# One overflow block of a mixture of experts moved from the end of the last stage to its start

## The chip, the cores and the metric

The kernel runs on one core of a Trainium2 chip. The metric is the device time of the whole kernel in microseconds (us). The engines are named as in the profile: PE is TensorE (PEld its weight loads), DVE is VectorE, ACT is ScalarE, POOL is GpSimd, SP is SyncE, which here only issues DMAs.

## What is computed

The kernel runs four pairs of attention and feed-forward layers on x, which is 2 batches of 1024 tokens of 256 numbers. Only the last feed-forward layer, a mixture of experts, is touched. Cut to what matters, it is:

```python
E, C, D, H = 8, 320, 256, 1024
xf = layernorm(x).reshape(2048, D)
eid = argmax(softmax(xf @ router_w + router_b), axis=-1)     # one expert for each token
rank = (cumsum(one_hot(eid), axis=0)[arange(N), eid] - 1)    # how many tokens before it chose the same expert
valid = rank < C                                             # an expert has room for 320 tokens
buf[eid, rank] = xf where valid
h = relu(einsum('ecd,edh->ech', buf, w1) + b1)
y = einsum('ech,ehd->ecd', h, w2) + b2
yov = relu(xf @ ow1 + ob1) @ ow2 + ob2                       # the tokens past 320 use this "overflow" network
out = where(valid, y[eid, rank], yov)
x = x + out
```

## The kernel before, in words

The tokens are held in SBUF as 16 tiles of 128 rows (the kernel calls a row of a tile with its token number, mean and reciprocal deviation behind it XW = 260 words). All of it is one program, stage after stage; the stage of this case is the last one, the function `moe3`. Its parts are written per engine, and each engine runs its part in the order written; semaphores tie them together. There is no scheduler.

**Routing.** The first twelve tiles (LAST = 12) are routed in earlier stages: their expert, their rank and their slot in a DRAM table `expert_rows` (`c.xd`) are known when the last stage starts. POOL has written the first eight of them into the table by then; at the head of the stage it writes tiles 8 to 11, one indirect DMA each (`scatter_tile`). The last four tiles must first be routed: PE transposes them (`ln_transpose`), multiplies them with the router's weights (`pe_logits`, L1172), brings the result back (`pe_logits_back`, L1181) and counts earlier tokens of each expert with bfloat16 matmuls of a matrix of ones (`pe_earlier_ranks`, `pe_count`, L1200; `pe_ranks`, L1215). DVE turns them into slots (`first_expert`, `slots`), and POOL then writes tiles 12 to 15. The table has 8 times 320 rows for the experts, and behind them, from row OV0 = 2560, rows for the overflow tokens of all experts, in the order of the tokens.

**The experts.** When all 16 scatters have landed, SP loads the table back (`load_x`, L2719, and `load_third`, L2725), then the second expert's weights (`load_w1`, `load_w2`), biases, more rows, the overflow rows (L2737) and the overflow network's weights `ow1` and `ow2` (L2740, L2741). PE runs nine matmuls whose result nobody reads (`keep_warm`, L110), transposes the rows (`x_transpose`, L2950) and then does for each of the eight experts `hidden` (L2963) and `outputs` (L2977), and after every second one `third_outputs` (L2986). ACT applies relu in between, DVE adds bias and residual (`finish`), POOL writes the result rows to the output in DRAM by an indirect DMA (`write`, L2769).

**The overflow blocks.** Behind the experts the overflow rows are computed in blocks of 128. A block is one `over_step` on PE: 16 matmuls with `ow1` (L3014), the next block's transposes (`over_transpose`, L2993) and 8 matmuls with `ow2` (L3025); DVE normalizes (`over_normal`, L2852), copies the transposed rows (`over_copy`, L2857) and finishes (`over_finish`); ACT does relu (`over_hidden`, L2914); POOL writes (`write_over`, L2781). Block 0 is written out in the program, and a loop with a count read at run time (`nbi`) does the rest, at least one more.

A matmul of float32 stands in the trace as two records: the 16 matmuls with `ow1` are 32 records.

Of the kernel before, what the change touches and what calls it, by code (L numbers as in the profile page):

```python
# [1146 lines left out]
def slots(c, dve, r, u, ranks, chain, read, nth=1):  # L1147
# [73 lines left out]
def scatter_tile(c, r, k):  # L1221
# [3 lines left out]
                                   in_=c.x[:, i * XW:(i + 1) * XW], in_offset=None).then_inc(c.scat, 16)  # L1225
# [1434 lines left out]
def moe3(c, d):  # L2660
# [4 lines left out]
    nbi = sb(c, "x_nbi", [1, 1], I32)  # L2665
    w1 = [c.early_w1, sb(c, "x_w11", [P, KC, HF])]
# [19 lines left out]
             "oy_set", "o_seen", "oy_ok", "o_out")  # L2686
# [15 lines left out]
    with nc.Block() as block:  # L2702
        @block.sync
        def _(sp):
# [3 lines left out]

            def load_w1(e):
# [16 lines left out]
            sp.wait_ge(c.scat, 16 * NT)  # L2726
# [6 lines left out]
            sp.dma_start(ob2[:, :], d["L3_ffn_ob2"].partition_broadcast(P)).then_inc(s["b_in"], 16)  # L2733
# [25 lines left out]
        def _(pool):  # L2759
# [4 lines left out]
            for k in range(LAST, NT):  # L2764
                scatter_tile(c, rt, k)
# [6 lines left out]
            for e in range(E3):  # L2772
                for r in range(2):
                    write(chunk(e, r), X[e % 4][:, r, D:D + 1].bitcast(U32))
                if e % 2 == 1:
                    write(third(e // 2), X3[e // 2 % 2][:, D:D + 1].bitcast(U32))

# [6 lines left out]
            write_over(0)  # L2784
            pool.wait_ge(s["nb_ok"], 1)
            nb = pool.value_load(nbi[0:1, 0:1], min_val=2, max_val=OVB)
            with pool.Fori(1, nb) as n:
# [409 lines left out]
```

## Time and profile before

| | before |
|---|---|
| runs (us) | 1004.54, 1004.16, 1007.02; median 1004.54 |
| the profiled execution: its time | 1005.3 us |
| its span, first to last instruction | 1003.5 us |
| mean granted clock of PE over the span | 0.968 |
| PE busy | 899.9 us, 90% of the span |
| last stage, from PE's first transposes | 803.4 to 1003.5 us |

The time of a run holds 1.8 us more than the span of the instructions. Times in the trace count from the span's start. The granted clock is the share of TensorE's full 2.4 GHz that was let through: 1.00 is 2.4 GHz and 0.50 is 1.2 GHz.

### The profile page before, as it was taken

How to read it: one execution, taken by the hardware profiler on the slowest of the kernel's cores; microseconds unless marked ns; L12 is line 12 of the kernel's file. 1: busy time of each engine (PE TensorE's matmuls, PEld its weight loads, DVE VectorE, ACT ScalarE, POOL GpSimd, SP SyncE). 2: the span in 40 equal slices, each digit the busy share in tenths (PEclk: the TensorE clock that was granted, in tenths of full speed). 3: DMA queues.
4: the chain of work that ended last, by engine and by line, in shares of the span. 5: the costliest groups of instructions: out<-in, count | busy, mean ns of one | idle time of the engine just before them, and what ended most of it. 6: DMA issues, size and time to landing. Idle time of an engine off the chain costs nothing. (4 is left out here: it accounts for less than half of the span.)

```text
span 1003.5 us, 17466 instructions
## 1 busy us (share of the span) xinstructions
PE 899.9 (90%) x5857; PEld 642.7 (64%) x5864; DVE 669.8 (67%) x1572; ACT 420.8 (42%) x1134; POOL 375.3 (37%) x279
## 2 busy tenths in 40 slices
PE   2899989999889995868899979999999949999997
PEld 2687744444478873744378647777777727778786
DVE  5899968889689988876377698787767531222221
ACT  2566641000146555752455336565655512122222
POOL 1776403333476732506545503333333430111111
PEclk9999999999899997987999999999999969999999
DMA  6100079999400007202356392311110149534200
GB/s 210 59 1 0 1 199 306 319 313 311 170 1 1 0 1 190 87 0 92 112 169 203 91 332 73 112 54 51 51 51 26 43 157 318 190 110 141 93 12 20
DMA packets 87259, 117.17 MB, mean 117 GB/s; under 512 B 12464, under 2 KB 75949, under 8 KB 86781
## 3 DMA queue, kind: packets, MB, share of 16 engines
q1 hardware_dynamic: 77455, 88.15, 29.1%
q10 hardware_dynamic: 4408, 15.46, 4.4%
q0 software_dynamic: 5328, 12.70, 3.5%
q8 instruction: 38, 0.62, 0.3%
q14 instruction: 30, 0.25, 0.1%
HBM read 68.08 MB, written 50.16 MB: 118 GB/s over the span
## 5 line engine op out<-in xcount | busy, mean ns | idle before, releaser
L1016 PE MATMUL psum<-m_W,lnT 128*128 128x512 f32 x256 | 114.2, 598 | 0.7 <-DVE acc L928 0.7
L410 POOL TENSOR_TENSOR prob<-prob,a_rden 128x1232 f32<-128x1232 f32 x30 | 67.5, 2249 | 58.4 <-DVE a_rden L506 58.4
L1016 PEld LDWEIGHTS psum<-m_W,lnT 128*128 128x128 f32 x256 | 47.2, 190 | 59.0 <-issue 56.5
L2907 ACT ACTIVATE prob<-psum,x_b 128x320 f32<-128x320 f32 x64 | 33.7, 527 | 117.1 <-PE psum L2963 117.1
L2574 PE MATMUL psum<-g_VW,pT 128*128 128x256 f32 (+1 forms) x320 | 72.5, 382 | 1.6 <-ACT pT L2461 1.5
L1001 POOL TENSOR_TENSOR m_masked<-m_rel,m_mrow 128x1232 f32<-128x1232 f32 x16 | 41.8, 2614 | 82.9 <-DMA masked_bias<-m_masked 62.0
L2769 POOL DMA_INDIRECT out_x<-x_yt,x_X x20 | 19.8, 991 | 135.3 <-DVE x_yt L2846 135.3
L2574 PEld LDWEIGHTS psum<-g_VW,pT 128*128 128x128 f32 (+1 forms) x320 | 59.5, 190 | 11.2 <-issue 3.7
L2232 POOL TENSOR_TENSOR g_qr<-g_t 128x1024 f32<-128x1024 f32 x15 | 35.4, 2359 | 71.1 <-DVE g_t L2305 71.1
L2239 POOL TENSOR_TENSOR prob<-prob,g_rden 128x1232 f32<-128x1232 f32 x15 | 33.7, 2247 | 67.6 <-DVE g_rden L2340 67.6
L2524 PE MATMUL psum<-g_Wq,lnT 128*128 128x512 f32 x128 | 58.0, 596 | 0.7 <-ACT lnT L2435 0.7
L1387 POOL DMA_INDIRECT routed_results<-pT,m_idx x39 | 38.3, 983 | 40.3 <-issue 23.5
L401 POOL TENSOR_SCALAR ln<-x_tiles,mean,rstd 128x256 f32<-128x256 f32 x32 | 41.4, 1294 | 30.6 <-DVE rstd L433 27.8
L2453 ACT ACTIVATE prob<-prob,mx 128x77 f32<-128x77 f32 x128 | 44.1, 347 | 19.0 <-DVE mx L2326 19.0
L472 DVE TENSOR_TENSOR prob<-psum,mx 128x616 f32<-128x616 f32 x64 | 48.2, 795 | 3.0
L466 DVE TENSOR_REDUCE mx<-psum 128x16 f32<-128x1232 f32 x32 | 45.6, 1424 | 4.7 <-PE psum L632 3.7
L962 ACT ACTIVATE lnT<-lnT_all 128x256 f32<-128x256 f32 x16 | 6.5, 415 | 95.2 <-PE psum L1023 95.2
L931 DVE SCALAR_TENSOR_TENSOR acc<-psum,gates,acc 128x256 f32<-128x256 f32 x96 | 40.3, 477 | 9.0 <-PE psum L1016 9.0
L549 ACT ACTIVATE prob<-prob 128x616 f32<-128x616 f32 x64 | 42.8, 713 | 6.1 <-DVE prob L472 6.1
L503 DVE TENSOR_REDUCE den<-prob 128x16 f32<-128x1232 f32 x30 | 42.8, 1427 | 3.6 <-ACT prob L549 3.2
L2843 DVE TENSOR_TENSOR x_yt<-psum,x_b 128x256 f32<-128x256 f32 (+1 forms) x24 | 10.2, 424 | 52.3 <-PE psum L2977 41.3
L1382 POOL DMA_INDIRECT routed_rows<-x_tiles,m_slot x32 | 31.8, 994 | 34.5 <-DVE m_slot L1575 25.3
(464 smaller groups left out, 2235.6 us busy)
## 6 DMA issues: line engine op xcount, KB each, us to landing
routed_rows<-hole SPq DMA_DIRECT2D x8, 2210.0 KB, 33.5
masked_bias<-m_masked ACTq DMA_DIRECT2D x16, 616.0 KB, 7.5
g_bias<-masked_bias SPq DMA_DIRECT2D x16, 616.0 KB, 3.8
m_xb<-routed_rows SPq DMA_DIRECT2D x39, 130.0 KB
m_rel<-in_rel_bias ACTq DMA_DIRECT2D x8, 616.0 KB, 9.6
expert_rows<-hole SPq DMA_DIRECT2D x1, 4680.0 KB, 32.4
g_early_w<-in_L_ffn_w SPq DMA_DIRECT2D x8, 512.0 KB, 4.6
g_early_w<-in_L_ffn_w SPq DMA_DIRECT2D x4, 1024.0 KB, 5.9
```

The lines of the kernel that those rows point to most:

```text
L401: nc.gpsimd.tensor_scalar(c.ln[b][:, :], xt(c, i), mean_of(c, i), rstd_of(c, i), ALU.subtract, ALU.mult).then_inc(ln_ok, 1)
L410: nc.gpsimd.tensor_tensor(heads(c.prob[b]), heads(c.prob[b]), rden[b][:, :].unsqueeze(2).to_broadcast([P, H, SK]), ALU.mult).then_inc(norm ...
L466: nv.reduce_max(c.mx[:, :].rearrange("p (r h) -> p r h", r=GROUPS), sview.rearrange("p r (h k) -> p r h k", k=SK), AX).then_inc(mx_ok, 1)
L472: nv.tensor_tensor(c.prob[b].rearrange("p (r h k) -> p r h k", r=GROUPS, k=SK)[:, r], sview[:, r].rearrange("p r (h k) -> p r h k", k=SK), ...
L503: nv.reduce_sum(c.den[:, :], heads(c.prob[b]), AX).then_inc(den_ok, 1)
L549: na.activation(c.prob[b][:, cols], c.prob[b][:, cols], ACT.Exp, scale=scale).then_inc(exp_ok, 1)
L931: ins = nv.scalar_tensor_tensor(out=c.acc[o][:, :], in0=src, scalar=gate, in1=c.acc[o][:, :], op0=ALU.mult, op1=ALU.add)
L1001: nc.gpsimd.tensor_tensor(masked[i % 2][:, :, :], rel[i // 2 % 2][:, :, :], mrow[:, i % 2, :].unsqueeze(1).to_broadcast([P, HB, SK]), ALU. ...
L1016: last = nt.matmul(c.ps[p][:, :], c.lnT[b][:, k * P:(k + 1) * P], W[:, k, p * 512:(p + 1) * 512], start=(k == 0), stop=(k == KC - 1))
L2453: last = na.activation(p, p, ACT.Exp, bias=c.mx[:, h:h + 1], accum_out=c.den[:, h:h + 1])
L2524: last = nt.matmul(c.ps[3 + u][:, :], c.lnT[b][:, k * P:(k + 1) * P], Wq[:, k, u * 512:(u + 1) * 512], start=(k == 0), stop=(k == KC - 1))
L2574: last = nt.matmul(bank_y[:, 0:D], c.pT[b][0:w, j * P:(j + 1) * P], VW[0:w, i // HALF, j, :], start=(j == 0), stop=(j == NB - 1))
```

## The change

The first overflow block is computed ahead of the experts. Its 128 rows are loaded into a tile of its own, `Xe`, as soon as the first twelve tiles are in the table; the last four tiles count on a semaphore of their own. The overflow network's weights and the bias `ob2` are loaded at the head of the stage. So that the first block is closed when tiles 12 to 15 are placed, PE also counts the experts' tokens in the first twelve tiles (12 more small matmuls; all its counts of earlier tiles now stand ahead of the logits), and DVE works out how many of the block's 128 rows they leave free (`free`); the overflow rows of the last four tiles begin behind the block (`start`). The matmuls of `keep_warm` at this place are gone. The loop of the other blocks begins at block 2, behind a block 1 that is written out, so at least three blocks are computed.

```diff
@@ -1157,9 +1157,9 @@
...
-    chain(nv.tensor_tensor(slotf, slotf, over, ALU.subtract))
+    chain(nv.scalar_tensor_tensor(out=slotf, in0=slotf, scalar=free, in1=over, op0=ALU.subtract, op1=ALU.subtract))
     chain(nv.scalar_tensor_tensor(out=slotf, in0=rank, scalar=float(CAP), in1=slotf, op0=ALU.is_lt, op1=ALU.mult))
-    return nv.scalar_tensor_tensor(out=r.slot[:, ones8], in0=slotf, scalar=float(E3 * CAP), in1=over, op0=ALU.add, op1=ALU.add)
+    return nv.scalar_tensor_tensor(out=r.slot[:, ones8], in0=slotf, scalar=start, in1=over, op0=ALU.add, op1=ALU.add)
...
     for shift in shifts:
-        pe_count(c, r, u, bank, shift, max(lo, shift), min(lo + wide, lo + shift), start=shift == shifts[0])
+        last = pe_count(c, r, u, bank, shift, max(lo, shift), min(lo + wide, lo + shift), start=shift == shifts[0])
+    if wide > n:
+        for j in range(lo):
+            last = c.nc.tensor.matmul(bank[:, wide * 8:(wide + 1) * 8], r.onesb, r.ohb[:, j * 8:(j + 1) * 8],
+                                      start=False, stop=True, skip_group_check=True)
+    return last
...
             sp.dma_start(ob1[:, :], d["L3_ffn_ob1T"]).then_inc(s["w_in"], 16)
+            sp.dma_start(ob2[:, :], d["L3_ffn_ob2"].partition_broadcast(P)).then_inc(s["w_in"], 16)
+            for k in range(KC):
+                sp.dma_start(ow1[:, k, :], d["L3_ffn_ow1"][k * P:(k + 1) * P, :]).then_inc(s["ow_in"], 16)
+            sp.dma_start(ow2[:, :, :], d["L3_ffn_ow2"].rearrange("(m p) n -> p m n", p=P)).then_inc(s["ow_in"], 16)
...
-            sp.wait_ge(c.scat, 16 * NT)
+            sp.wait_ge(c.scat, 16 * LAST)
+            sp.dma_start(Xe[:, :], xd[OV0:OV0 + P, :]).then_inc(s["first_in"], 16)
+            sp.wait_ge(s["scat"], 16 * (NT - LAST))
             load_x(0)
             load_third(0)
...
-            sp.dma_start(ob2[:, :], d["L3_ffn_ob2"].partition_broadcast(P)).then_inc(s["b_in"], 16)
...
                          xd[OV0:OV0 + OVX * P, :].rearrange("(r p) n -> p r n", p=P)).then_inc(s["ox_in"], 16)
-            for k in range(KC):
-                sp.dma_start(ow1[:, k, :], d["L3_ffn_ow1"][k * P:(k + 1) * P, :]).then_inc(s["ow_in"], 16)
-            sp.dma_start(ow2[:, :, :], d["L3_ffn_ow2"].rearrange("(m p) n -> p m n", p=P)).then_inc(s["ow_in"], 16)
...
-                scatter_tile(c, rt, k)
+                scatter_tile(c, rt, k, s["scat"])
...
-            for e in range(E3):
-                for r in range(2):
...
             write_over(0)
+            for e in range(E3):
+                for r in range(2):
...
+
+            write_over(1)
             pool.wait_ge(s["nb_ok"], 1)
-            nb = pool.value_load(nbi[0:1, 0:1], min_val=2, max_val=OVB)
-            with pool.Fori(1, nb) as n:
+            nb = pool.value_load(nbi[0:1, 0:1], min_val=3, max_val=OVB)
+            with pool.Fori(2, nb) as n:
...
             dve_rstd(c, dve, chain, s["ve_ok"], s["std_ok"])
+            dve.wait_ge(s["early_ps"], 1)
+            chain(nv.tensor_scalar(over8[:, :], bank_rank[:, (NT - LAST + 1) * 8:(NT - LAST + 2) * 8], -float(CAP), 0.0, ALU.add, ALU.max))
+            chain(nv.reduce_sum(free[:, 0:1], over8[:, :], AX))
+            chain(nv.tensor_scalar(free[:, 0:1], free[:, 0:1], -1.0, float(P), ALU.mult, ALU.add))
+            nv.tensor_scalar(start[:, :], free[:, 0:1], 0.0, float(OV0), ALU.max, ALU.add)
+            chain(nv.tensor_scalar(free[:, 1:2], free[:, 0:1], 0.0, None, ALU.max))
...
+            slots(c, dve, rt, 2, bank_rank, chain, s["pre_read"], 1, free[:, 1:2], start[:, 0:1]).then_inc(s["slot_ok"], 1)
+            dve.wait_ge(s["w_in"], 16 * 4)
...
+            chain(nv.tensor_tensor(nbf[:, 0:1], nbf[:, 0:1], start[0:1, :], ALU.add))
...
+            nv.tensor_scalar(nbi[:, :], nbf[:, 1:2], 3.0, None, ALU.max).then_inc(s["nb_ok"], 1)
...
-            def over_rows(n):
-                return Xo[:, ds(n * XW, D)]
+            def over_rows(n, at=0, wide=D):
+                return Xe[:, at:at + wide] if is_static(n) and n == 0 else Xo[:, ds(n * XW + at, wide)]
...
+            def over_finish(n):
+                dve.wait_ge(s["oy_ps"], n + 1)
...
+            dve.wait_ge(s["first_in"], 16)
+            over_normal(0)
+            over_copy(0)
             normal_rows(0)
             x_copy(0)
+            over_finish(0)
             for e in range(E3):
                 if e + 1 < E3:
...
-                    over_normal(0)
-                    over_copy(0)
+                    over_normal(1)
+                    over_copy(1)
...
-            over_step(0)
-            nb = dve.value_load(nbi[0:1, 0:1], min_val=2, max_val=OVB)
-            with dve.Fori(1, nb) as n:
+            over_step(1)
+            nb = dve.value_load(nbi[0:1, 0:1], min_val=3, max_val=OVB)
+            with dve.Fori(2, nb) as n:
                 over_step(n)
...
-            act.wait_ge(s["w_in"], 16 * 3)
-            for e in range(E3):
-                if e >= 2:
-                    wait(act, s["y_ps"], third(e // 2 - 1) + 1)
...
+            act.wait_ge(s["w_in"], 16 * 4)
...
             over_hidden(0)
+            for e in range(E3):
+                if e >= 2:
...
+            over_hidden(1)
             act.wait_ge(s["nb_ok"], 1)
-            nb = act.value_load(nbi[0:1, 0:1], min_val=2, max_val=OVB)
-            with act.Fori(1, nb) as n:
+            nb = act.value_load(nbi[0:1, 0:1], min_val=3, max_val=OVB)
+            with act.Fori(2, nb) as n:
...
                 ln_transpose(n, k)
+            pe_earlier_ranks(c, rt, 2, bank_rank).then_inc(s["early_ps"], 1)
             pe.wait_ge(s["lnT_ok"], NT - LAST)
             pe_logits(c, rt, 2, bank_lg).then_inc(s["lg_ps"], 1)
             pe.wait_ge(s["lgT_ok"], 1)
             pe_logits_back(c, rt, 2, bank_back).then_inc(s["logits_ps"], 1)
-            pe_earlier_ranks(c, rt, 2, bank_rank)
...
@@ -2968,6 +2990,8 @@
                 b = e % 2
                 if e > 0:
                     pe.wait_ge(w2_in[b], 16 * ((e + 1) // 2))
+                if e == 0:
+                    pe.wait_ge(s["oy_ok"], 1)
...
-            pe.wait_ge(c.scat, 16 * NT)
-            keep_warm(c, c.ps[3], 9)
-            x_transpose(0)
-            for e in range(E3):
-                hidden(e)
-                if e + 1 < E3:
...
-                    over_transpose(0)
-                outputs(e)
...
-            pe.wait_ge(s["ow_in"], 16 * (KC + 1))
-
             def over_step(n):
+                early = is_static(n) and n == 0
...
-                over_transpose(n + 1)
+                if not early:
+                    over_transpose(n + 1)
                 wait(pe, s["oy_ok"], n)
-                if is_static(n):
+                if is_static(n) and not early:
...
+            over_transpose(0)
+            pe.wait_ge(s["ow_in"], 16 * (KC + 1))
             over_step(0)
+            x_transpose(0)
+            for e in range(E3):
+                hidden(e)
+                if e + 1 < E3:
...
+                    over_transpose(1)
+                outputs(e)
...
+            over_step(1)
             pe.wait_ge(s["nb_ok"], 1)
-            nb = pe.value_load(nbi[0:1, 0:1], min_val=2, max_val=OVB)
-            with pe.Fori(1, nb) as n:
+            nb = pe.value_load(nbi[0:1, 0:1], min_val=3, max_val=OVB)
+            with pe.Fori(2, nb) as n:
                 over_step(n)
```

On PE at the start of the stage stand before the change (names: `lnT_all` the transposed tiles, `qT` here the router's weights, `oT` the logits, `lg` the tokens' choices, `choice` the matrix of ones):

```order
L1172 MATMUL psum<-lnT_all,qT 32x256 x4
L1181 MATMUL psum<-ident,oT 128x64 x2
L1200 MATMUL psum<-lg,choice 128x40 x8
L1200 MATMUL psum<-lg,choice 128x8
L1200 MATMUL psum<-lg,choice 128x16
```

and after it, at the same place:

```order
L1200 MATMUL psum<-lg,choice 128x16
L1200 MATMUL psum<-lg,choice 128x8
L1212 MATMUL psum<-lg,choice 128x8 x12
L1172 MATMUL psum<-lnT_all,qT 32x256 x4
L1181 MATMUL psum<-ident,oT 128x64 x2
L1220 MATMUL psum<-lg,choice 128x32
```

The counts of earlier tiles (16 matmuls) have moved from behind the logits to ahead of them, and 12 more follow them (L1212).

A little further on PE, between the ranks and the first expert, stand before the change (`RQ,identb` is `keep_warm`, `x_XL` the experts' normalized rows, `x_xT` the same transposed, `g_early_w` the first expert's weights, `prob` its hidden layer):

```order
L1200 MATMUL psum<-lg,choice 128x8
L110 MATMUL psum<-RQ,identb 128x512 x9
L2950 MATMUL psum<-ident,x_XL 128x128 x6
L2963 MATMUL psum<-x_xT,g_early_w 128x320 x16
L2950 MATMUL psum<-ident,x_XL 128x128 x4
```

and after it (`oT` are now the overflow block's rows, `x_ow` its weights, `Wall` its hidden layer):

```order
L1200 MATMUL psum<-lg,choice 128x8
L3017 MATMUL psum<-ident,oT 128x128 x2
L3025 MATMUL psum<-oT,x_ow 128x128 x16
L3037 MATMUL psum<-x_ow,Wall 128x256 x8
L2972 MATMUL psum<-ident,x_XL 128x128 x6
L2985 MATMUL psum<-x_xT,g_early_w 128x320 x16
```

The block has taken the place of the nine `keep_warm` matmuls, between the ranks and the first expert's transposes.

SP issues these DMAs from the head of the stage before the change (`x_X` are the experts' rows, `x_w` the second expert's weights, `x_tiles` here the tile of the overflow rows):

```order
L2705 DMA x_steps<-in_c_steps 1x14
L2706 DMA x_b<-in_L_ffn_b1T 128x64
L2707 DMA x_ob<-in_L_ffn_ob1T 128x8
L2719 DMA x_X<-expert_rows 128x2x260
L2725 DMA x_X<-expert_rows 64x260 x2
L2719 DMA x_X<-expert_rows 128x2x260
L2711 DMA x_w<-in_L_ffn_w 128x1024 x2
L2715 DMA x_w<-in_L_ffn_w 128x8x256
L2732 DMA x_b<-in_L_ffn_b 128x2048
L2733 DMA x_ob<-in_L_ffn_ob 128x256
```

and after it:

```order
L2712 DMA x_steps<-in_c_steps 1x14
L2713 DMA x_b<-in_L_ffn_b1T 128x64
L2714 DMA x_ob<-in_L_ffn_ob1T 128x8
L2716 DMA x_ob<-in_L_ffn_ob 128x256
L2718 DMA x_ow<-in_L_ffn_ow 128x1024 x2
L2719 DMA x_ow<-in_L_ffn_ow 128x8x256
L2739 DMA x_Xe<-expert_rows 128x260
L2731 DMA x_X<-expert_rows 128x2x260
L2737 DMA x_X<-expert_rows 64x260 x2
L2731 DMA x_X<-expert_rows 128x2x260
```

The overflow network's bias and weights stand ahead of all loads of rows, and the load of the block's rows ahead of the experts' first.

## Rows read from the trace of the kernel before

**Rows 1.** The page: busy time, share of the span, number of instructions.

```profile
PE 899.9 (90%) x5857; PEld 642.7 (64%) x5864; DVE 669.8 (67%) x1572; ACT 420.8 (42%) x1134; POOL 375.3 (37%) x279
```

**Rows 2.** Waits of 796 to 840 us: who waited for what, us, times, longest.

```profile
DVE x_XL L2823 <- DMA x_X<-expert_rows: 9.3, 1, 9.3
PE psum L110 <- DMA expert_rows<-x_tiles,acc: 8.4, 1, 8.4
```

**Rows 3.** Timeline of PE, stage start: start us, us busy, what, idle before it.

```profile
803.41 1.32 PE L2932 MATMUL psum<-ident,x_tiles 128*128 128x128 f32 x8 [1.62 <-PEq L175]
805.20 1.71 PE L1172 MATMUL psum<-lnT_all,qT 128*32 128x256 f32 x8 [0.47 <-ACT lnT_all L2896]
807.79 0.64 PE L1200 MATMUL psum<-lg,choice 128*128 128x40 bf16 x16
...
818.22 3.62 PE L110 MATMUL psum<-RQ,identb 128*128 128x512 bf16 x8 [8.36 <-DMA expert_rows<-x_tiles,acc]
822.75 0.88 PE L2950 MATMUL psum<-ident,x_XL 128*128 128x128 f32 x6 [0.91 <-DVE x_XL L2823]
...
840.99 8.78 PE L2963 MATMUL psum<-x_xT,x_w 128*128 128x320 f32 x32
```

**Rows 4.** The chain that ended last, in order of time, same place.

```profile
815.34 2.43 DMA expert_rows<-x_tiles,acc
...
818.75 2.77 DMA x_X<-expert_rows
821.63 1.07 DVE x_XL L2823 x3
```

**Rows 5.** Timeline of PE, end of the kernel: the overflow blocks.

```profile
968.25 3.84 PE L3014 MATMUL psum<-oT,x_ow 128*128 128x128 f32 x32
...
982.84 3.73 PE L3014 MATMUL psum<-oT,x_ow 128*128 128x128 f32 x32
986.41 0.38 PE L2993 MATMUL psum<-ident,oT 128*128 128x128 f32 x2
986.63 3.62 PE L3025 MATMUL psum<-x_ow,Wall 128*128 128x256 f32 x16
990.08 3.73 PE L3014 MATMUL psum<-oT,x_ow 128*128 128x128 f32 x32
```

**Rows 6.** Timeline of POOL and DVE, stage start and last block.

```profile
807.81 0.96 POOL L1224 DMA_INDIRECT expert_rows<-x_tiles,acc  x1 [0.31 <-issue]
...
812.18 0.14 DVE L2808 TENSOR_SCALAR x_nbi<-x_nbf 1x1 int32<-1x1 f32 x1
...
991.67 0.41 DVE L2852 TENSOR_SCALAR oT<-x_tiles 128x256 f32 x1 [0.23 <-issue]
...
994.07 0.42 DVE L2857 COPY oT<-psum 128x256 f32<-128x256 f32 x1 [2.00 <-PE psum L2993]
997.62 0.42 DVE L2877 TENSOR_TENSOR qT<-psum,x_ob 128x256 f32<-128x256 f32 x1 [3.12 <-PE psum L3025]
...
998.25 0.43 DVE L2881 TENSOR_TENSOR qT<-qT,x_tiles 128x256 f32<-128x256 f32 x1
```

**Rows 7.** Timeline of SP's queue: issues of DMAs.

```profile
804.09 0.42 SPq L2707 DMA_DIRECT2D x_ob<-in_L_ffn_ob1T  x1
...
820.02 0.94 SPq L2711 DMA_DIRECT2D x_w<-in_L_ffn_w  x2
821.01 0.43 SPq L2715 DMA_DIRECT2D x_w<-in_L_ffn_w  x1
...
822.49 0.88 SPq L2733 DMA_DIRECT2D x_ob<-in_L_ffn_ob  x1
```

**Rows 8.** DMA issues, 803 to 842 us, then 618 to 650 us: KB each, us to landing.

```profile
x_w<-in_L_ffn_w SPq DMA_DIRECT2D x1, 1024.0 KB, 8.5
...
g_early_w<-in_L_ffn_w SPq DMA_DIRECT2D x1, 1024.0 KB, 6.4
```

**Rows 9.** L2769's 20 indirect DMAs, then L2719's 8 loads, min/median/max.

```profile
DMA to landing us min/median/max: 2.1/2.4/5.9
...
DMA to landing us min/median/max: 2.7/8.3/10.3
```

**Rows 10.** Windows: length, busy of PE, PEld, DVE, ACT, POOL; PE's granted clock, DMA share, GB/s.

```profile
805.20:809.90 4.70, 3.05 (x31) 1.54 (x31) 1.75 (x11) 0.43 (x2) 2.88 (x3) 0.53 0.33 117
809.90:818.20 8.30, 0.00 (x0) 0.13 (x2) 2.08 (x14) 0.00 (x0) 3.83 (x4) 0.50 0.18 65
818.20:822.50 4.30, 3.62 (x8) 1.06 (x7) 0.87 (x3) 0.00 (x0) 0.00 (x0) 0.50 0.78 214
822.50:825.00 2.50, 0.92 (x7) 0.71 (x7) 1.53 (x6) 0.00 (x0) 0.00 (x0) 0.99 0.95 326
```

More of the change, by code:

```diff
@@ L1144, in first_expert, with slots @@
     return nv.tensor_tensor(tiles(hot), tiles(tmp), wide(first), ALU.is_equal)
-def slots(c, dve, r, u, ranks, chain, read, nth=1):
+def slots(c, dve, r, u, ranks, chain, read, nth=1, free=0.0, start=float(E3 * CAP)):
     nv = c.nc.vector
@@ L1218, in pe_ranks, with scatter_tile @@
     return last
-def scatter_tile(c, r, k):
+def scatter_tile(c, r, k, done=None):
     i = TOKEN_ORDER[k]
     c.nc.gpsimd.indirect_dma_start(out=c.xd, out_offset=bass.IndirectOffsetOnAxis(ap=r.slot[:, k:k + 1], axis=0),
-                                   in_=c.x[:, i * XW:(i + 1) * XW], in_offset=None).then_inc(c.scat, 16)
+                                   in_=c.x[:, i * XW:(i + 1) * XW], in_offset=None).then_inc(done or c.scat, 16)
 def row_statistics(c, u):
@@ L2665, in moe3 @@
     nbi = sb(c, "x_nbi", [1, 1], I32)
+    over8, free, start = sb(c, "x_over8", [P, 8]), sb(c, "x_free", [P, 2]), sb(c, "x_start", [P, 1])
+    Xe = sb(c, "x_Xe", [P, XW])
     w1 = [c.early_w1, sb(c, "x_w11", [P, KC, HF])]
@@ L2784, in _ @@
             write_over(0)
+            for e in range(E3):
+                for r in range(2):
+                    write(chunk(e, r), X[e % 4][:, r, D:D + 1].bitcast(U32))
+                if e % 2 == 1:
+                    write(third(e // 2), X3[e // 2 % 2][:, D:D + 1].bitcast(U32))
+            write_over(1)
             pool.wait_ge(s["nb_ok"], 1)
-            nb = pool.value_load(nbi[0:1, 0:1], min_val=2, max_val=OVB)
-            with pool.Fori(1, nb) as n:
+            nb = pool.value_load(nbi[0:1, 0:1], min_val=3, max_val=OVB)
+            with pool.Fori(2, nb) as n:
                 write_over(n)
@@ L2857, in over_copy @@
                 nv.tensor_copy(xTo[:, :], c.ps[0][:, 0:D]).then_inc(s["oT_ok"], 1)
+            def over_finish(n):
+                dve.wait_ge(s["oy_ps"], n + 1)
+                wait(dve, s["o_out"], n * 16)
+                nv.tensor_tensor(yo[:, :], c.ps[6][:, 0:D], ob2[:, :], ALU.add).then_inc(s["oy_set"], 1)
+                nv.tensor_copy(ido[:, :], over_rows(n, D, 1).bitcast(U32))
+                wait(dve, s["o_seen"], n)
+                dve.wait_ge(s["oy_set"], n + 1)
+                nv.tensor_tensor(yo[:, :], yo[:, :], over_rows(n), ALU.add).then_inc(s["oy_ok"], 1)
+            dve.wait_ge(s["first_in"], 16)
+            over_normal(0)
+            over_copy(0)
             normal_rows(0)
             x_copy(0)
+            over_finish(0)
             for e in range(E3):
@@ L2873, in _ @@
                     finish(third(e // 2), [(e - 1, slice(0, C2)), (e, slice(C2, P))], rows_of(e - 1, 2))
-            def over_finish(n):
-                dve.wait_ge(s["oy_ps"], n + 1)
-                wait(dve, s["o_out"], n * 16)
-                nv.tensor_tensor(yo[:, :], c.ps[6][:, 0:D], ob2[:, :], ALU.add).then_inc(s["oy_set"], 1)
-                nv.tensor_copy(ido[:, :], Xo[:, ds(n * XW + D, 1)].bitcast(U32))
-                wait(dve, s["o_seen"], n)
-                dve.wait_ge(s["oy_set"], n + 1)
-                nv.tensor_tensor(yo[:, :], yo[:, :], over_rows(n), ALU.add).then_inc(s["oy_ok"], 1)
             def over_step(n):
@@ L2900, in _ @@
             logits_copy(c, rt, 2, bank_lg).then_inc(s["lgT_ok"], 1)
-            act.wait_ge(s["w_in"], 16 * 3)
-            for e in range(E3):
-                if e >= 2:
-                    wait(act, s["y_ps"], third(e // 2 - 1) + 1)
-                for m in range(MH):
-                    act.wait_ge(s["h_ps"], e * MH + (m + 1))
-                    na.activation(hT[e % 2][:, m, :], c.ps[2 + m % 4][:, 0:CAP], ACT.Relu,
-                                  bias=b1[:, e * MH + m:e * MH + m + 1]).then_inc(s["h_ok"], 1)
+            act.wait_ge(s["w_in"], 16 * 4)
             def over_hidden(n):
@@ L2917, in _ @@
             over_hidden(0)
+            for e in range(E3):
+                if e >= 2:
+                    wait(act, s["y_ps"], third(e // 2 - 1) + 1)
+                for m in range(MH):
+                    act.wait_ge(s["h_ps"], e * MH + (m + 1))
+                    na.activation(hT[e % 2][:, m, :], c.ps[2 + m % 4][:, 0:CAP], ACT.Relu,
+                                  bias=b1[:, e * MH + m:e * MH + m + 1]).then_inc(s["h_ok"], 1)
+            over_hidden(1)
             act.wait_ge(s["nb_ok"], 1)
-            nb = act.value_load(nbi[0:1, 0:1], min_val=2, max_val=OVB)
-            with act.Fori(1, nb) as n:
+            nb = act.value_load(nbi[0:1, 0:1], min_val=3, max_val=OVB)
+            with act.Fori(2, nb) as n:
                 over_hidden(n)
```

21 lines of the change are left out of this document (7 added, 14 removed).

## The prediction

> **What bounds the kernel now.** I read the page first: PE is busy for 90% of the span [rows 1], so the question is where PE is not busy, and what PE does that could be done there. The waits around the start of the last stage show the hole: PE waits 8.4 us for the scatters into the table, and DVE 9.3 us for the rows loaded back [rows 2]. The timeline shows it from PE's side: after the ranks (about 809.9) PE does nothing until `keep_warm` at 818.22, and that is work nobody reads; the first transposes of the experts start at 822.75 [rows 3]. The chain of the end says why: the last scatter starts at 815.34 and lands 2.43 us later, the last load starts at 818.75 and lands 2.77 us later, DVE normalizes for 1.07 us, and PE goes on [rows 4]. From there to the end PE waits for nobody for long. At the end it computes four overflow blocks, one every 990.08 - 982.84 = 7.24 us [rows 5]. So the kernel's end is PE's work from 822.75 on: a block taken from there is worth 7.24 us, less what it pushes 822.75 back.
>
> **The removed block.** The trace has four blocks: the first of `ow1`'s groups is at 968.25, the last at 990.08, (990.08 - 968.25) / 7.24 = 3 steps after the first [rows 5]. So between 385 and 512 tokens overflow. The change fills its block only if the first twelve tiles alone overflow by 128 or more; rows they leave free would be added to the rest, and a fifth block would come. Counting the choices of the reference's router on its inputs gives 472 overflow tokens, 215 of them in the first twelve tiles. The first block is then full, nothing is left free, and (472 - 128) / 128 rounds up to 3 blocks behind the experts. Term one: **-7.24 us**. Block 1 takes block 0's place in the program and the tail behind the last block stays what it was.
>
> **Moved and added counts.** PE now does the 16 counts of earlier tiles and 12 more ahead of the logits. 16 took 0.64 us [rows 3], so 28 take 28 x 0.04 = 1.12 us. They start when the tiles' transposes end, at 803.41 + 1.32 = 804.73, and end at 805.85, where the logits started at 805.20: 0.65 us late. Before, the 16 lay in PE's wait for DVE and cost nothing. DVE waits for PE's logits behind them, then come the slots, POOL's four scatters, SP's loads: all 0.65 us late. The five new small DVE instructions (about 0.2 us each, like the one at 812.18 [rows 6] and its neighbours) stand ahead of that wait, while DVE would wait anyway, and cost nothing. So the experts' rows let PE begin at 822.75 + 0.65 = 823.4 at the earliest. Term two is this 0.65 us only if the block is done by then.
>
> **When the block can start.** It needs its rows and its weights. SP is free at 804.09 + 0.42 = 804.51; the bias takes 0.88 us to issue, `ow1` 0.94, `ow2` 0.43 [rows 7] (by DMAs of the same shape elsewhere), so `ow2` is issued from about 806.4. A 1 MB load behind others of its kind lands 8.5 us after its issue, one with little ahead of it 6.4 us [rows 8]: 812.8 to 814.9. I take 8.5 us, since the bias and 1 MB of `ow1` are right ahead: 814.9. Tile 12's scatter starts at 807.81 [rows 6] and lands 2.43 us later [rows 4] at 810.2 if the weights leave it alone. SP issues the load of the block's rows (0.4 us), which takes 2.77 us [rows 4]: 813.4 alone. It is behind `ow2` in SP's queue, so I take 815.0. DVE has finished its counts by 812.18 + 0.14 + 0.65 = 813.0 [rows 6] and is no limit. Then 0.1 us to wake DVE, 0.41 us to normalize [rows 6], 0.05 us to PE: PE transposes from 815.6.
>
> **How long it takes there.** At the end of the kernel the block costs 7.24 us because its transposes and copy hide under the block before. Here they don't: from the start of the transposes to the end of the copy it is 994.07 + 0.42 - 993.65 = 0.84 us (the transposes at 993.65 are 7.24 us behind those at 986.41 [rows 5]; the copy is in [rows 6]). I add 0.3 us for the wake-up and the slower clock: `ow1` starts at 816.7. The rest is 986.41 - 982.84 = 3.57 us and 990.08 - 986.63 = 3.45 us, 7.02 us at full clock [rows 5]. But PE has idled, and its granted clock is 0.50 (1.2 GHz) from 805.2 to 822.5; it rose to 2.4 GHz 4.3 us after `keep_warm` began [rows 10]. The same 4.3 us from 815.6 give 819.9. From 816.7 to 819.9 PE does 3.2 / 2 = 1.6 us of the 7.02; the other 5.42 us end at 825.3. Then the experts' transposes start, their rows long there: 825.3 - 822.75 = 2.55 us later than before. Term two is therefore **+2.55 us**, and the 0.65 us are inside it. `keep_warm` needs no replacement: the block warms the clock itself.
>
> **What is free.** `ow1`, `ow2` and `ob2` in SP's later queue are gone, which only frees DMA. The second expert's weights now land at about 821.01 + 8.5 + 0.65 = 830.2 [rows 7, 8] and are wanted after 840.99 [rows 3]. DVE finishes the block between the first expert's copy and the second's rows: 998.25 + 0.43 - 997.62 = 1.06 us [rows 6], with the second expert's transposes wanted some 9 us later. The first expert's `outputs` wait for this finish, also some 9 us later; POOL writes the block while it has nothing else. ACT's relu of the block lies under PE's matmuls as it does at the end.
>
> **The sum.** -7.24 + 2.55 = -4.7 us, of which I give 0.2 for wake-ups I have not counted: -4.5. On the profiled execution's own time of 1005.3 us that is 1000.8; it was 0.8 us above the median of 1004.54, so against the median I say 1000.0.
>
> The loads at the head speak against this change. The nearest row is POOL's writes to the output, of which the slowest took 5.9 us to land and the median 2.4 [rows 9], the slow one among heavy loads; by it tile 12 lands at 813.7, the rows at 816.9 and not 815.0, and 1.9 us of the gain are lost, -2.6 us. The Trainium skill (DMA: Bandwidth & Descriptors, Issuing engines are not separate DMA queues) says that DMAs of all issuing engines run on the same 16 DMA engines and interleave, and its section on queues, rings and completion order that a DMA engine takes the queues in turn, packet by packet. By that a scatter gets its turn beside the weights: my estimate from the page is at most twice its 2.43 us, tile 12 at 812.7, the rows at 815.9, and a sum of -3.6 us.
>
> **The rivals.**
> - *The block hides almost whole.* The weights land after 6.4 us, scatter and load as if alone: rows at 813.4, 1.6 us sooner, block done at 823.7 against the 823.4 of the experts' own rows. -7.24 + 0.95 = -6.3 us: 998.2 (997.9 if only the 0.65 us are left). For it: the DMA share is only 0.33 at 805.2 to 809.9 [rows 10]. Against it: 2 MB are added just there. 0.14.
> - *Rows or clock late.* The slow scatter above, or a clock that rises later: were it at 1.2 GHz during the whole block, the block would take 14.0 us to 830.7, and the sum would be +0.7 us. Between: 0 to -3 us, 1001.6 to 1004.5, say 1002.5. For it: the block's transposes and the wait for the copy are thinner work than `keep_warm`. 0.20.
> - *Slower: the block's rows are stuck behind the weights.* Loads from the table took up to 10.3 us, 8.3 in the median, when the queue was full [rows 9]. It decides where the rows land after 815.0 + (7.24 - 2.55) = 819.7, for then PE has lost more at the front than it saved at the end; with a scatter of 5.9 and a load of 10.3 us they land at 807.81 + 5.9 + 0.4 + 10.3 = 824.4, +4.7 us: 1009.3. Against it: such loads stood in a queue that kept the DMA engines 0.95 busy [rows 10], and this one has 2 MB ahead of it. 0.08, half of it by over 0.3%.
> - *The change does not do what it says*: five blocks in all, so +2.55 us: 1007.1. The counts above speak against it. 0.02.
> - My forecast, -3 to -6 us: 0.56.
>
> **The numbers.** 0.3% is 3.0 us, about what can be told from no change. Faster by more than that are the forecast and the first rival: 0.70. Within it the second and half of the third: 0.24. Slower 0.06. The range from 998.2 to 1003.6 leaves out the end of the first rival, the slow third of the second and the last two.
>
> **What would show it.** Right: three groups of `ow1` matmuls at the end, 7.24 us apart, and one of about 5 us between 816 and 822, in which the spacing halves half-way; the block's rows landing at about 815; the first experts' transposes at about 825.3, hidden work 2.2 us behind as before. Wrong: PE waiting for the block's rows beyond 817 (scatter or load late), or for the weights with the rows transposed; a granted clock of 0.50 into the `ow2` matmuls; four groups still at the end; a wait of PE in the first two experts, which would mean that DVE's or POOL's new order costs something.

## The result, and the profile after

The changed kernel takes 1001.39 us in the median of 20 runs, the kernel before 1006.46 us in as many: a ratio of 0.9958, 95% interval 0.9944 to 0.9971. That is 4.2 us less (2.9 to 5.6); the two medians by themselves lie 5.1 us apart, which is inside this interval. The trace's own execution took 999.59 us, with a span of 997.8 us.

Single runs of one kernel differ by several us here (before: 1001.4 to 1010.3), and part of that arises before the last stage. The two traces differ by 5.7 us in their spans, but 4.2 us of it are there when the last stage begins: PE's first transposes of the stage are at 803.41 before [rows 3] and at 799.17 after. That difference comes in earlier, where nothing was changed: PE's work of the same name is 0.3 us apart in the two traces at 467 us, 4.24 us at 580.6 us, and it stays so from there on. So below, times are given as distances from the stage's first transposes, which I call the stage's start. By that the first pair of traces says: last stage 200.1 us before, 198.6 us after, a gain of 1.5 us only.

The waits around the start of the last stage, after (us in total, times, longest):

```profile
PE psum L3017 <- DVE oT L2869: 9.5, 1, 9.5
...
DVE oT L2869 <- DMA x_Xe<-expert_rows: 6.4, 1, 6.4
```

PE's wait of [rows 2] is no shorter; it has a new cause, DVE's normalizing of the early block, and behind that the load of its rows. PE's timeline of the same trace, against [rows 3]:

```profile
799.17 1.32 PE L2954 MATMUL psum<-ident,x_tiles 128*128 128x128 f32 x8 [1.63 <-PEq L175]
...
800.33 0.55 PE L1200 MATMUL psum<-lg,choice 128*128 128x40 bf16 x16
...
800.74 0.44 PE L1212 MATMUL psum<-lg,choice 128*128 128x8 bf16 x12
...
801.11 1.06 PE L1172 MATMUL psum<-lnT_all,qT 128*32 128x256 f32 x8
...
814.44 0.69 PE L3017 MATMUL psum<-ident,oT 128*128 128x128 f32 x2 [9.48 <-DVE oT L2869]
...
815.74 5.37 PE L3025 MATMUL psum<-oT,x_ow 128*128 128x128 f32 x32 [0.61 <-DVE oT L2874]
820.94 3.62 PE L3037 MATMUL psum<-x_ow,Wall 128*128 128x256 f32 x16
824.40 0.82 PE L2972 MATMUL psum<-ident,x_XL 128*128 128x128 f32 x6
```

The experts' first transposes are 824.40 - 799.17 = 25.2 us behind the stage's start, where they were 822.75 - 803.41 = 19.3. I call this distance the front; it has grown by 5.9 us. Why the block starts late is in the timelines of POOL, SP and DVE:

```profile
803.58 0.96 POOL L1229 DMA_INDIRECT expert_rows<-x_tiles,acc  x1 [0.30 <-issue]
...
810.11 0.33 SPq L2739 DMA_DIRECT2D x_Xe<-expert_rows  x1
...
813.97 0.41 DVE L2869 TENSOR_SCALAR oT<-x_Xe 128x256 f32<-128x256 f32 x1 [6.38 <-DMA x_Xe<-expert_rows]
...
818.58 1.06 DVE L2840 TENSOR_SCALAR x_XL<-x_X 128x256 f32<-128x256 f32 x3 [2.99 <-DMA x_X<-expert_rows]
```

The block's rows wait for the last of the first twelve tiles. (The prediction calls it tile 12; counted from 0, as in the kernel, it is tile 11. I call it the twelfth tile.) Its scatter starts at 803.58, 4.4 us behind the stage's start as in [rows 6], but SP, which waits for it, issues its load only at 810.11. The chain that ended last has the two durations:

```profile
803.58 6.52 DMA expert_rows<-x_tiles,acc
...
810.11 3.84 DMA x_Xe<-expert_rows
```

The scatter took 6.5 us where 2.43 [rows 4] had done. The experts' own rows are there at 818.58 + 1.06 = 819.6 and wait almost 5 us for PE. The windows (busy of PE, PEld, DVE, ACT, POOL, then granted clock, DMA share, GB/s) put the block's two halves at the two clocks:

```profile
810.00:814.00 4.00, 0.00 (x0) 0.00 (x0) 0.03 (x1) 0.00 (x0) 1.23 (x2) 0.50 0.73 260
...
814.00:819.00 5.00, 3.95 (x17) 3.58 (x18) 1.23 (x4) 0.00 (x0) 0.00 (x0) 0.50 0.65 181
819.00:824.40 5.40, 5.40 (x36) 4.94 (x35) 0.63 (x2) 2.28 (x8) 0.00 (x0) 1.00 0.92 317
```

And the end, against [rows 5], has three blocks where there were four, 7.35 and 7.25 us apart:

```profile
969.83 3.84 PE L3025 MATMUL psum<-oT,x_ow 128*128 128x128 f32 x32
...
977.18 3.73 PE L3025 MATMUL psum<-oT,x_ow 128*128 128x128 f32 x32
...
984.43 3.73 PE L3025 MATMUL psum<-oT,x_ow 128*128 128x128 f32 x32
```

From the experts' first transposes to the end it is 1003.5 - 822.75 = 180.8 us before and 997.8 - 824.40 = 173.4 us after. I call this the rest. Rest -7.4, front +5.9: -1.5 us. The question for the experiments was where the other 2.7 us of the timed 4.2 are.

### The profile page after: what moved, and what is told of

Same layout as the page of the kernel before. It is cut to its first block and busy times, and to the rows that moved or that the text cites. A ratio compares the mean times of both kernels' runs of the same rounds, so it can differ in the third digit from the quotient of the medians.

```text
span 997.8 us, 17467 instructions
## 1 busy us (share of the span) xinstructions
PE 896.7 (90%) x5867; PEld 644.1 (65%) x5867; DVE 668.5 (67%) x1577; ACT 420.4 (42%) x1134; POOL 375.3 (38%) x279
## 5 line engine op out<-in xcount | busy, mean ns | idle before, releaser
L1392 POOL DMA_INDIRECT routed_results<-pT,m_idx x39 | 38.4, 984 | 39.3 <-DVE pT L1725 19.8
L931 DVE SCALAR_TENSOR_TENSOR acc<-psum,gates,acc 128x256 f32<-128x256 f32 x96 | 40.6, 476 | 10.8 <-PE psum L1016 10.7
L660 PE MATMUL psum<-pT,a_VB 128*32 128x128 f32 x1088 | 40.9, 275 | 3.4 <-ACT pT L555 3.4
```

## The experiments

All ratios are to the kernel before, timed on the same chip. Front and rest come from each kernel's own trace.

| kernel | front | rest | last stage | ratio (95%) |
|---|---|---|---|---|
| before | 19.3 | 180.8 | 200.1 | 1 |
| before_again | 18.5 | 184.1 | 202.5 | 0.9992 (0.9972 to 1.0012) |
| before_third | 19.3 | 180.8 | 200.0 | 0.9994 (0.9971 to 1.0018) |
| changed | 25.2 | 173.4 | 198.6 | 0.9958 (0.9944 to 0.9971) |
| after_again | 24.9 | 173.4 | 198.3 | 0.9964 (0.9947 to 0.9981) |
| after_third | 24.8 | 173.4 | 198.2 | 0.9954 (0.9932 to 0.9976) |
| weights_first | 18.8 | 183.7 | 202.5 | 1.0000 (0.9985 to 1.0014) |
| one_fewer | 19.4 | 175.2 | 194.6 | 0.9933 (0.9909 to 0.9957) |
| before_warm_long | 19.4 | 182.5 | 201.9 | 0.9990 (0.9971 to 1.0009) |
| warm | 25.0 | 173.3 | 198.3 | 0.9949 (0.9929 to 0.9970) |
| warm_long | 24.8 | 173.4 | 198.2 | 0.9965 (0.9934 to 0.9996) |
| swap | 23.3 | 173.4 | 196.7 | 0.9946 (0.9927 to 0.9965) |
| swap_again | 22.2 | 173.5 | 195.7 | 0.9946 (0.9920 to 0.9972) |
| swap_warm | 22.4 | 175.9 | 198.3 | 0.9951 (0.9930 to 0.9973) |

### The two kernels again

*before_again* and *before_third* are the kernel before, *after_again* and *after_third* the changed kernel, with no edit.

> The kernel before, unchanged, for a second trace. The first pair of traces puts 1.5 us of the gain in the last stage (200.1 us before, 198.6 us after, from PE's first transposes of the stage to the end) and 4.2 us ahead of it, in stages that the change does not touch. Theory 1 (the stages ahead differ from execution to execution whatever the kernel): ratio 1.000; the last stage again 200.1 us within 0.5, the stages ahead up to 4 us away from 803.4. Theory 2 (the last stage itself varies, by the phase of the clock or the landing of the scatters): the last stage differs by 1 us or more from 200.1.

> The changed kernel, unchanged, for a second trace. Theory 1 (the front of the last stage is always lengthened by 5.9 us, so the stage gains 1.5 us, and what the medians show beyond that comes from ahead of the stage): last stage 198.6 us within 0.5, first transposes of the experts 25.2 us behind the stage's. Theory 2 (the front varies; the first trace shows a bad case): that distance between 22 and 25 us, last stage 196 to 198 us. Ratio to before 0.996 in both.

> The kernel before, unchanged, for a third trace. Theory A (the nine matmuls of keep_warm and the thin work behind them do not hold the clock at 1.00 through the first expert in every execution): the part from the experts' first transposes to the end is 182.5 to 184 us in this one, as in four of the five traces so far that have keep_warm and four blocks or one fewer (taken with 7.24 us more), and the last stage lasts 202 us or so. Rival (the first trace is the usual case): 180.8 us and 200.1 us. Ratio 1.000.

> The changed kernel, unchanged, for a third trace. Theory A: the part from the experts' first transposes to the end is 173.3 to 173.4 us again, since a whole block of dense work stands ahead of them, and the front is 24.9 to 25.3 us. Rival (that it was at full clock each time is chance): over 174.5 us. Ratio 0.996.

For the changed kernel theory 1 was right: its stage is steady (198.6, 198.3, 198.2) and its front too. For the kernel before both theories hold: its last stage began at 799.8 us in the second trace and at 803.4 in the other two, and its length varies (200.1, 202.5, 200.0), which was theory 2. In the first trace, the first expert's hidden layer:

```profile
824.96 8.85 PE L2963 MATMUL psum<-x_xT,g_early_w 128*128 128x320 f32 x32 [1.34 <-DVE x_xT L2832]
```

The second trace, timeline of PE (cut off at 832 us, so with 31 of the 32 records):

```profile
813.53 4.02 PE L110 MATMUL psum<-RQ,identb 128*128 128x512 bf16 x9 [8.10 <-DMA expert_rows<-x_tiles,acc]
818.25 1.54 PE L2950 MATMUL psum<-ident,x_XL 128*128 128x128 f32 x6 [0.70 <-DVE x_XL L2823]
821.13 11.17 PE L2963 MATMUL psum<-x_xT,g_early_w 128*128 128x320 f32 x31 [1.33 <-DVE x_xT L2832]
```

and its windows:

```profile
817.00:822.00 5.00, 2.97 (x10) 1.85 (x9) 2.85 (x9) 0.00 (x0) 0.00 (x0) 0.50 0.98 331
822.00:826.00 4.00, 4.00 (x8) 2.49 (x8) 0.00 (x0) 0.76 (x2) 0.00 (x0) 0.50 1.07 400
826.00:828.00 2.00, 2.00 (x8) 1.46 (x7) 0.00 (x0) 0.82 (x2) 0.00 (x0) 0.91 0.98 256
```

`keep_warm` ran, and yet the clock stayed at 0.50 until after 826: the transposes took 1.54 us instead of 0.88, the first expert's whole hidden layer 11.4 us instead of 8.85. The experts' rows were early in this execution (front 18.5, not 19.3), but the rest is 3.3 us longer. In the third trace the clock was up in time again, so my expectation of a low clock there was a miss. The changed kernel's rest is 173.4 us in all three; a whole block of dense matmuls stands ahead of its first expert, which I take for the reason, though no run isolates it.

### The weights alone at the head

```diff
             sp.dma_start(ob1[:, :], d["L3_ffn_ob1T"]).then_inc(s["w_in"], 16)
+            for k in range(KC):
+                sp.dma_start(ow1[:, k, :], d["L3_ffn_ow1"][k * P:(k + 1) * P, :]).then_inc(s["ow_in"], 16)
+            sp.dma_start(ow2[:, :, :], ...).then_inc(s["ow_in"], 16)
...
-            for k in range(KC):
-                sp.dma_start(ow1[:, k, :], ...)
-            sp.dma_start(ow2[:, :, :], ...)
```

> The kernel before with one part of the change: the overflow network's weights loaded at the head of the stage (the bias stays where it was); the four blocks stay at the end. Theory 1 (2 MB at the head hold up the scatters): the scatter of the twelfth tile lands 6 us after its start instead of 2.4, the last one up to 2 us later than before, and the experts' first transposes start 1 to 2 us later; ratio 1.001 to 1.002. Rival (the scatters of the last four tiles come when the weights are nearly through): no delay, ratio 1.000.

The ratio is 1.0000 (0.9985 to 1.0014). The last scatters are through at the same time: SP issues the experts' first load 13.8 us behind the stage's start, in before_again 13.7. The rival was right: by themselves the weights cost the kernel before nothing that shows, 0.3 us of front at most (18.8 against 18.5). What it waits for is the last of the 16 scatters, and that starts at 810.98, when the weights are nearly through (`ow2` lands at 811.3), and takes 2.7 us. What they cost the changed kernel is the early block's own rows, which come while they are under way. This trace, too, has the first expert's beginning at the low clock (again 31 of its 32 records):

```profile
818.62 1.54 PE L2950 MATMUL psum<-ident,x_XL 128*128 128x128 f32 x6 [0.92 <-DVE x_XL L2823]
821.49 10.87 PE L2963 MATMUL psum<-x_xT,g_early_w 128*128 128x320 f32 x31 [1.33 <-DVE x_xT L2832]
```

### One block fewer

The kernel before without its last block; 88 overflow tokens are not computed.

```diff
-            nv.tensor_scalar(nbi[:, :], nbf[:, 1:2], 2.0, None, ALU.max).then_inc(s["nb_ok"], 1)
+            nv.tensor_scalar(nbi[:, :], nbf[:, 1:2], -1.0, 2.0, ALU.add, ALU.max).then_inc(s["nb_ok"], 1)
```

> The kernel before with one overflow block fewer behind the experts: the count of the run-time loop is lowered by one, so the last block (88 of the 472 overflow tokens) is left out. Theory (a block at the end is worth its whole 7.24 us): the part from the experts' first transposes to the end shrinks by 7.2 to 7.3 us, ratio 0.9928. Rival (part of the block hides under the tail of POOL's writes or under the experts): less than 6.5 us, ratio above 0.9935.

The ratio of 0.9933 is 6.7 us less (4.3 to 9.1), and holds 7.24. The rest is 175.2 us, 5.5 us less than the first trace's, not 7.2: here the clock fell back to 0.50 for some 3.4 us inside the first expert, whose hidden layer took 10.5 us and not 8.85:

```profile
828.17 10.54 PE L2963 MATMUL psum<-x_xT,g_early_w 128*128 128x320 f32 x32 [1.33 <-DVE x_xT L2832]
```

The blocks at the end of this trace are 7.24 us apart, and one is gone:

```profile
980.50 3.73 PE L3014 MATMUL psum<-oT,x_ow 128*128 128x128 f32 x32
...
987.74 3.73 PE L3014 MATMUL psum<-oT,x_ow 128*128 128x128 f32 x32
```

### Idle PE kept busy

*warm* (the changed kernel) and *swap_warm* (below) have the first piece, *warm_long* both, *before_warm_long* the second alone.

```diff
+            pe.wait_ge(c.scat, 16 * LAST)
+            keep_warm(c, c.ps[3], 9)
             over_transpose(0)
...
             pe_ranks(c, rt, 2, bank_rank).then_inc(s["pre_ps"], 1)
+            keep_warm(c, c.ps[3], 20)
```

> The changed kernel with nine matmuls that nobody reads put between the first twelve tiles' landing and the early block, where PE is idle. Theory 1 (the block is slowed by the clock of 0.50 in its first 4.6 us): the block's matmuls run at 1.00 almost from the start, it ends 1.6 to 2.3 us sooner against the stage's start, and the time falls by as much, ratio to before about 0.994. Rival (the block's end is set by weights that land late): the block ends where it did and the ratio stays at 0.996.

> The kernel before with 20 matmuls that nobody reads right behind the ranks, where PE waits 8 us for the scatters; the nine of keep_warm stay. Theory A (what the gain shows beyond 1.5 us is that the kernel before starts its first expert at the low clock in part of its executions, as its second trace shows, 21.4 to 26.4 us behind the stage's start, and the changed one never does): with PE busy the clock is at 1.00 before the first expert in every execution; the part from the experts' first transposes to the end is 180.8 us or less, never 184, and the ratio is 0.997 to 0.999. Rival (that second trace is rare): the ratio is 1.000.

> The changed kernel with 20 matmuls that nobody reads right behind the ranks and nine more when the first twelve tiles have landed. Theory (the early block is slow only by the clock of 0.50 in its first 3.4 to 4.8 us): the clock does not fall or is back at 1.00 before the block, the ow1 matmuls take 3.7 us instead of 5.4 to 5.7, the experts' first transposes start 22.8 to 23.3 us behind the stage's start instead of 24.9 to 25.2, ratio 0.994. Rival (the clock falls in spite of it, or the 20 matmuls at the low clock delay the block): 24.9 us or more, ratio 0.996 or above.

None of the three did what I wanted. In *warm* the nine matmuls filled the last 4 us of the gap and the clock rose no sooner: at about 20.0 us behind the stage's start (799.56), 19.8 in the changed kernel. Its windows:

```profile
808.00:812.00 4.00, 1.70 (x5) 0.59 (x6) 0.00 (x0) 0.00 (x0) 3.02 (x4) 0.50 1.05 384
812.00:816.00 4.00, 3.39 (x10) 1.31 (x9) 0.84 (x2) 0.00 (x0) 0.00 (x0) 0.50 0.38 117
816.00:819.00 3.00, 3.00 (x16) 3.00 (x16) 0.66 (x3) 0.00 (x0) 0.00 (x0) 0.50 0.90 251
819.00:820.00 1.00, 1.00 (x8) 1.00 (x8) 0.40 (x2) 0.57 (x3) 0.00 (x0) 0.72 0.91 344
```

The front is 25.0 us as without them. The expectation's rival, weights that land late, is not the reason either: `ow2`, issued at 802.31, landed 10.4 us later, at 812.7, and PE's first matmul with the weights is at 815.58. The ratio of 0.9949 overlaps that of the changed kernel, so it is no gain that I can show. In *warm_long* the block ran at the full clock (`ow1` in 3.65 us), but the result of PE's logits reached ACT 2.5 us late in that trace and the 29 matmuls, done at 820.8, stood in front of the block: front 24.8, no gain. *before_warm_long* had the clock up before the first expert, and then lost it during the expert, right behind the two waits of 2.52 and 1.33 us for the rows: rest 182.5, and a ratio of 0.9990. So theory A's first half stands (the kernel before has its first expert partly at the low clock in three of the five traces without the 20 matmuls, and in this one), and my remedy for it fails. That the waits right ahead of the expert would have to be filled instead is what this suggests; it was not tried.

### The two sets of weights exchanged

The stage before has room for one set of weights in advance, and used it for the first expert. Here the overflow network's get it, and the first expert's are loaded in the last stage, behind the early block's rows.

```diff
-                sp.dma_start(c.early_w1[:, k, :], d["L3_ffn_w1"][k * P:(k + 1) * P, :]).then_inc(c.early_in, 16)
+                sp.dma_start(c.early_w1[:, k, :], d["L3_ffn_ow1"][k * P:(k + 1) * P, :]).then_inc(c.early_in, 16)
...
-    w1 = [c.early_w1, sb(c, "x_w11", [P, KC, HF])]
-    ow1, ow2 = sb(c, "x_ow1", [P, KC, HF]), sb(c, "x_ow2", [P, MH, D])
+    w1 = [sb(c, f"x_w1{u}", [P, KC, HF]) for u in range(2)]
+    ow1, ow2 = c.early_w1, c.early_w2
...
             sp.dma_start(Xe[:, :], xd[OV0:OV0 + P, :]).then_inc(s["first_in"], 16)
+            load_w1(0)
+            load_w2(0)
```

> The changed kernel with the two sets of weights exchanged: the overflow network's are loaded in the stage before, in the place of the first expert's, and the first expert's are loaded in the last stage right behind the block's rows. Theory (the rows of the block are late because the 2 MB at the head delay the scatter of tile 12 from 2.4 to 6.5 us and the load from 2.8 to 3.8): the load is issued 6.9 to 7.1 us behind the stage's start instead of 10.7 to 10.9, DVE has the rows at 10.0 to 10.5 instead of 14.2 to 14.8, the block ends 3 to 4 us sooner, at 21 to 22, and the experts' first transposes follow there. If the first expert's weights are then in time, ratio 0.993; the rival is that they are not, or hold up the last scatters, and the experts start no sooner than 24 us, ratio 0.996.

> The kernel with the two sets of weights exchanged, unchanged, for a second trace and time. In its first trace the front was 23.3 us, and PE's results of the router reached DVE and ACT 2.8 us late, for which nothing in the trace accounts. If that is an accident of one execution, the logits' copy starts about 3.0 us behind the stage's start instead of 6.4; the front stays at 22.5 to 23.3 us, since the block's rows do not hang on it; ratio 0.994 to 0.995. If it is of this kernel, it comes again.

> The kernel with the two sets of weights exchanged and nine matmuls that nobody reads behind the landing of the first twelve tiles. Theory (in the exchanged kernel what is left of the front is the block at the low clock, 1.5 to 3 us): the block ends up to 2 us sooner, front 21 to 22.5 us, ratio 0.992 to 0.994. Rival (as in the kernel with nine such matmuls and the weights in the old order, the clock does not rise sooner for them): front 23.3 us, ratio as without them.

SP's queue in swap_again (stage's start 799.80):

```profile
806.67 0.33 SPq L2736 DMA_DIRECT2D x_Xe<-expert_rows  x1
807.04 0.91 SPq L2720 DMA_DIRECT2D x_w<-in_L_ffn_w  x2
807.99 0.43 SPq L2724 DMA_DIRECT2D x_w<-in_L_ffn_w  x1
817.13 0.38 SPq L2728 DMA_DIRECT2D x_X<-expert_rows  x1
```

and PE's timeline there:

```profile
809.23 0.69 PE L3012 MATMUL psum<-ident,oT 128*128 128x128 f32 x2 [3.63 <-DVE oT L2868]
810.53 6.33 PE L3020 MATMUL psum<-oT,g_early_w 128*128 128x128 f32 x32 [0.61 <-DVE oT L2873]
816.70 3.62 PE L3032 MATMUL psum<-g_early_w,Wall 128*128 128x256 f32 x16
822.04 0.88 PE L2971 MATMUL psum<-ident,x_XL 128*128 128x128 f32 x6 [1.73 <-DVE x_XL L2839]
```

With no weights under way the scatter of the twelfth tile has landed 6.9 us behind the stage's start instead of 10.7 to 10.9 (2.5 us after its start and not 6.3 to 6.5), and the load of the block's rows takes 2.1 us instead of 3.4 to 3.8, so their lateness is shown to be the weights'. The block starts at 9.4 us and is done at 20.5. Now the experts' own rows are last: their load is issued at 17.3 us, in the changed kernel at 15.0 to 15.2, because the first expert's weights hold up the last scatters in their turn: SP goes on 5.9 us after the start of the last one, in the changed kernel 3.8. The front is 22.2 us. In the first trace, *swap* (stage's start 808.58), the front is 23.3 us, and there the block sets it. Its rows had landed at 8.9 us as in swap_again, but DVE took them up only at 11.8, straight behind its counts for the router, which were late:

```profile
820.39 0.39 DVE L2868 TENSOR_SCALAR oT<-x_Xe 128x256 f32<-128x256 f32 x1
```

The late results of the router (they reached DVE 2.8 us late), seen in that trace and in warm_long's, did not come again in swap_again or swap_warm; their cause stays open. *swap_warm* fills the gap ahead of the block, which then runs at full clock and is done early; PE waits 3.16 us for the experts' rows, the clock falls and the first expert pays (rest 175.9). A dense block ahead of the expert does not help when such a wait lies between them.

This version takes 0.9946 of the kernel before's time in both timings. In the traces its stage is 1.7 to 2.7 us shorter than the changed kernel's mean of 198.4, but the intervals of the ratios overlap, so the timings do not separate the two; the 0.993 of the expectation was not reached.

## Why the prediction was right, point by point

The forecast was 1000.0 us against a median of 1004.54, -4.5 us; the timings say -4.2 (2.9 to 5.6). The number was right, in part by luck: of its two terms one was right and the other too small, and what made up for it was something that I had not seen.

- **-7.24 us for the block.** Right: three blocks 7.35 and 7.25 us apart instead of four, no fifth block, and one_fewer's 6.7 us (4.3 to 9.1).
- **The counts, 0.65 us.** Too high. The logits start 801.11 - 799.17 = 1.94 us behind the stage's start, 1.79 before [rows 3], since most of the 28 counts ran while PE would have waited for ACT. POOL's fifth scatter is at 7.6 us; it was at 8.1 in the first and third trace of before, which had the logits at the low clock, and at 7.35 in the second, which had them at the high one: 0.27 us, and hidden.
- **The rows' arrival, 11.7 us behind the stage's start** (815.1 in the prediction, with 0.1 to wake DVE). Mis-sized, and the step that failed: DVE had them at 14.8, 14.2 and 14.3 us, 2.5 to 3.1 us later. The scatter of the twelfth tile took 6.3 to 6.5 us in place of 2.43, some 4 us more. The prediction had allowed 4.8 us from there to the rows (0.4 for the issue, 2.77, and 1.6 for a queue behind `ow2`); it was 3.4 to 3.8, which gave 1.0 to 1.4 us back. This was the rival "rows or clock late". Its price, the slow write of [rows 9], puts the rows at 816.9, that is at 13.5 us, but leaves the 1.6 us out; with them it is 15.1. swap_again shows the cause, as it undoes just this.
- **The block's length with the clock.** Right: from its first transposes to the experts' 9.96, 10.3 and 10.0 us, 9.7 in the prediction. The clock rose 4.6, 5.3 and 4.7 us after PE began, 4.3 in the prediction. That 4.3 was misread: [rows 3] has 8 of the nine `keep_warm` matmuls, and the third trace, which has all nine, starts them 0.4 us sooner, so that it was 4.7. Nor is it a constant. In the two traces swap and swap_again, with the same block, the clock rose after 6.9 and 6.6 us, and over all runs between 2.6 us (warm_long) and 12.8 us (before_again) after PE began. `ow2` was no limit, though it landed 10.8 us after its issue and not 8.5.
- **The front.** +5.9 us against the first trace and not +2.55. With the first pair of traces alone the sum is -1.5 us and the forecast would have been wrong.
- **What I held for constant.** The price of the kernel before. I read one trace, in which `keep_warm` had the clock up in time. Among five traces with that front (before, before_again, before_third, weights_first, one_fewer) two have the first expert's beginning at the low clock, one a fall inside it. The two are those whose last stage began early, at 799.8 us, with the logits at the full clock (1.06 us); in the other three it began at 803.4 to 806.6, the logits ran partly at the low clock (1.67 to 1.92 us), and the clock was up again before the first expert. Five traces do not show that the one causes the other. With one block added to one_fewer their stages last 200.1, 202.5, 200.0, 202.5 and 201.8 us, 201.4 in the mean; the changed kernel's three 198.4. That is -3.0 us, at the edge of the timed interval.

The rest, between 3.0 and the timed 4.2 us, stays open. The spread of the stages ahead (the last stage starts at 799.2 to 803.4 us in the six traces of the two kernels) is as large as the effect, and six traces do not say whether it plays a part.

For the scatter the Trainium skill (DMA: Bandwidth & Descriptors, Queues, rings and completion order) says that each DMA engine takes its queues in turn, packet by packet, from which the prediction's estimate was at most twice the undisturbed 2.43 us. The trace does not agree with that estimate: it was 6.5 us, and the measurement decides. The Trainium skill (the same page, Latency and other measured facts) also says that an access to HBM takes 0.2 us on average and 2 us at high load. The DMA share was 0.98 to 1.15 in the half-microsecond windows from 805.5 to 811 of the changed kernel's first trace, so that fits, but no run here takes the two apart.

## What to carry to other kernels

When work is moved into a wait, look at what that work needs, not only at the wait: its own inputs (here rows through a scatter) were slowed by its own weights, issued just ahead of them. Load the weights of moved work before the transfers that it waits for, or behind them, but not on top; the traces of the exchanged weights gained 1.7 to 2.8 us of front over the changed kernel by that, too little for the timings to show. And before a price is put on a stage whose engine has been idle, take more than one trace: a clock that is up in time in one execution may be late in the next, and a dense piece of real work right ahead of the critical one can be worth more than the few matmuls that were put there to keep it up.

## What was not expected of the hardware

- An indirect scatter of 128 rows took 2.4 to 2.5 us to land with free DMA engines (before, swap_again) and 6.3 to 6.5 us with 2 MB of loads under way (the changed kernel); the 130 KB load behind it took 2.0 to 2.1 us and 3.4 to 3.8.
- Matmuls that nobody reads did not bring the clock up reliably. After 9 of them in 4.0 us it was at 0.50 for another 8.8 us (before_again, 817.55 to 826.35), in which PE waited for 0.7 and 1.33 us and was busy most of the rest; in before_third it was up 4.7 us after the start of the same nine.
- The clock fell from 1.00 to 0.50 while PE was inside a dense hidden layer (one_fewer, before_warm_long), less than 1 us behind its start, with waits of 0.7 to 2.5 and of 1.33 us just before it, and stayed there for some 3.4 us. It cost 1.7 us: 182.5 us for the rest (with the block added in one_fewer) against 180.8.
